# A selective-scan mixer kernel: old states enter through the first column of the products, most scans start from zero

## The chip, the cores and the metric

The kernel runs on one core of one Trainium2 chip. The metric is the device time of one execution in microseconds (us); the time before is the median of three executions. A trace of one further execution is what the rows below are read from.

The core has a matrix engine (TensorE, PE in the rows), a vector engine (VectorE, DVE), a scalar engine (ScalarE, ACT), GpSimd (POOL) and a queue that issues the transfers (SyncE, SP). Each runs its own instructions in the order in which they are written; semaphores make one wait for another.

## The reference

Three parts follow one another on an input of 4 sequences of 2048 tokens with 512 channels: a feed-forward part, the mixer, the same feed-forward part again, each with layer norm and a residual. The change lies in the mixer, cut here to what matters (D_INNER is 1024, D_STATE 16):

```
x, z = split((inp - mean(inp)) @ W_in)
x = silu(conv(x) + conv_b)
Bm, Cm = split(x @ W_x)
delta = softplus(x @ W_dt + b_dt)
def step(h, t):
    delta_t, B_t, C_t, u_t = t
    dA = exp(delta_t[:, :, None] * A[None, :, :])
    dBu = delta_t[:, :, None] * B_t[:, None, :] * u_t[:, :, None]
    h = dA * h + dBu
    y = einsum('bds,bs->bd', h, C_t)
out = ((y + x * D) * silu(z)) @ W_out
```

The state h (1024 channels by 16 states) is carried along the 2048 tokens of a sequence and starts at zero.

## The kernel before

The mixer cuts each sequence into 8 chunks of 256 tokens (T), so there are 32 chunks. A chunk has 8 blocks (ND) of 128 channels, which lie on the partitions, and a block has 4 units (NG) of 4 states (SG). A chunk is thus 32 units (NU), numbered n = 0 to 31; block b is units 4b to 4b+3. A unit is two pairs of states: the first pair (half 0) is scanned in place in PSUM, the second (half 1) is scanned from PSUM into SBUF (tile mx_hp).

What each engine does for a unit:

- ScalarE (decay, L1167) writes exp(delta * A) for a pair into one of three PSUM banks (mx_ps_da). A bank is free again when the pair three places earlier is done with: a first pair after VectorE has multiplied it by C (s_m2) and ScalarE has copied its last column to the state tile mx_hst (keep_psum, L1196), a second pair after its scan.
- GpSimd (times_b, L1009) writes delta*u*B for two units at a time into mx_dbu, which has room for four units (NM). So the products of units n and n+1 wait until unit n-3 is scanned.
- VectorE (scan, L1350) runs the recurrence along 256 tokens, four scans a unit, each starting from a column of mx_hst, or from the constant 0.0 in the first chunk of a sequence. It multiplies the first pair by C (times_c, L1363). It also does three taps of the convolution in each unit 4b (L1322) and the gating in each unit 4b+2 (L1330).
- GpSimd multiplies the second pairs of two units by C at once (times_c_sbuf, L1027; singly for the last four units), and per block adds two halves of delta (add_log, L996) and makes delta*u (delta_u, L1031).
- TensorE makes all products with weights and sums the states by transposes onto mx_ps_y.

For unit 4b+2 the first pair is different (on_pe): its products come from TensorE, and its decays go to mx_da_sb ahead of time.

All engines walk through the units with a written-out timetable. A list such as GATE_AT holds the unit at which the work for each block is due, counted from the chunk's unit 0, and the order in which the loops over due() stand is the order within that unit. Two silu visits a chunk, at units 5 and 21 (Z_SILU_AT), load the silu table, work on four blocks of z and of u, and load the exp table back (L1291, L1098, L1075, L1296). The B rows of the next chunk are loaded by SyncE in four transfers of 512 KB, one for each unit position g (spread, L900); the transfer for g is issued when the products of unit 28+g are made, and before the change unit 0 waits for g = 0 and 1 only.

## Time and profile before

| | |
|---|---|
| median of 3 executions | 5207.4 us (5206.98 to 5207.64) |
| the profiled execution's own time | 5209.97 us |
| its span in the trace | 5208.0 us |
| the mixer's chunks lie at | 715.0 to about 4598 us |
| busy over the span: PE, DVE, ACT, POOL | 94%, 87%, 74%, 72% |
| instructions | 83685 |

The busy shares are means over three parts. GpSimd is little used in the feed-forward parts and nearly always busy in the mixer, so the mixer has to be read by itself, chunk by chunk.

### The profile page before, as it was taken

The numbers are of one execution on the slowest core, as the hardware profiler recorded it, in microseconds if no ns is written. First come the engines' busy times: TensorE is split into PE (matmuls) and PEld (weight loads), VectorE is DVE, ScalarE is ACT, GpSimd is POOL, SyncE is SP. The second block draws the span as 40 slices with busy tenths as digits, with TensorE's granted clock in tenths as the row PEclk, the third lists the DMA queues.
The fourth block names the chain that finished last, engine by engine and source line by source line (L and its number), as shares of the span: only waits on it lengthen the run. The fifth ranks groups of instructions, "written<-read, shape, count | busy, mean of one in ns | idle before, by whom it ended". The sixth has DMA issues, their size and how long they took to land. (4 is left out here: it accounts for less than half of the span.)

```text
span 5208.0 us, 83685 instructions
## 1 busy us (share of the span) xinstructions
PE 4916.9 (94%) x25472; PEld 3971.2 (76%) x25472; DVE 4510.7 (87%) x7540; ACT 3849.1 (74%) x9976; POOL 3756.8 (72%) x1701
## 2 busy tenths in 40 slices
PE   8999989999999999999999999999999999979999
PEld 6777767777777777777777777777777777768887
DVE  6777669999999999999999999999899999977775
ACT  5556558888888888888888888888888888854443
POOL 1111059999999999999999999999999999931110
PEclk9999999999999999999999999999999999989999
DMA  3222231111111111111111111111111111211111
GB/s 83 91 80 81 102 110 46 46 46 48 58 53 55 46 46 46 46 46 46 46 51 54 46 46 54 58 54 50 46 46 46 46 46 46 66 58 53 65 57 41
DMA packets 154802, 292.21 MB, mean 56 GB/s; under 512 B 40688, under 2 KB 58096, under 8 KB 154352
## 3 DMA queue, kind: packets, MB, share of 16 engines
q1 hardware_dynamic: 154352, 286.82, 16.6%
q8 instruction: 208, 3.41, 0.3%
q14 instruction: 242, 1.98, 0.1%
HBM read 218.60 MB, written 68.18 MB: 55 GB/s over the span
## 5 line engine op out<-in xcount | busy, mean ns | idle before, releaser
L1009 POOL TENSOR_TENSOR mx_dbu<-mx_bs,mx_du 128x2048 f32<-128x2048 f32 (+2 forms) x513 | 2047.3, 3991 | 291.7 <-DVE mx_hp L1350 287.4
L1167 ACT ACTIVATE mx_ps_da<-mx_dl,mx_a 128x256 f32<-128x256 f32 x3584 | 1558.6, 466 | 72.9 <-DVE mx_hp L1350 39.9
L1350 DVE TENSOR_TENSOR_SCAN mx_hp<-mx_ps_da,mx_hst,mx_dbu 128x256 f32<-128x256 f32 x1792 | 1333.5, 744 | 215.3 <-ACT mx_ps_da L1167 213.6
L1027 POOL TENSOR_TENSOR mx_hp<-mx_hp,mx_cs 128x1024 f32<-128x1024 f32 (+1 forms) x576 | 1220.7, 2125 | 4.6 <-ACT mx_hst L1176 4.6
L1472 PE MATMUL mx_ps_m<-mx_u,mx_w_dt 128*128 128x256 f32 x4096 | 947.9, 385 | 93.6 <-ACT mx_duT L1148 67.8
L1350 DVE TENSOR_TENSOR_SCAN mx_ps_da<-mx_ps_da,mx_hst,mx_dbu 128x256 f32<-128x256 f32 x1344 | 937.9, 748 | 4.8 <-ACT mx_ps_da L1167 1.8
L1472 PEld LDWEIGHTS mx_ps_m<-mx_u,mx_w_dt 128*128 128x128 f32 x4096 | 759.6, 190 | 239.0 <-issue 136.2
L1363 DVE TENSOR_TENSOR mx_hc<-mx_ps_da,mx_cs 128x512 f32<-128x512 f32 x1024 | 696.0, 680 | 10.3 <-PE mx_ps_y L1502 8.3
L1502 PEld LDWEIGHTS mx_ps_y<-mx_ident,mx_hp 128*128 128x128 f32 x4096 | 511.0, 142 | 203.6 <-issue 114.8
L1502 PE MATMUL mx_ps_y<-mx_ident,mx_hp 128*128 128x128 f32 x4096 | 620.3, 274 | 8.4 <-POOL mx_hp L1027 8.4
L1502 PE MATMUL mx_ps_y<-mx_ident,mx_hc 128*128 128x128 f32 x4096 | 617.2, 273 | 4.1 <-DVE mx_gy L1330 3.9
L247 POOL TENSOR_TENSOR f_rstd<-f_ve,f_half 128x4 f32<-128x4 f32 x48 | 48.4, 1009 | 682.4 <-DVE f_ve L414 682.4
L1441 PE MATMUL mx_ps_m<-mx_hT,mx_w_in 128*128 128x259 f32 x2048 | 520.1, 399 | 5.9 <-POOL mx_ident L990 3.8
L1452 PE MATMUL mx_ps_m<-mx_hT,mx_w_in 128*128 128x256 f32 x2048 | 485.2, 379 | 4.4 <-DVE mx_u L1322 4.4
L1502 PEld LDWEIGHTS mx_ps_y<-mx_ident,mx_hc 128*128 128x128 f32 x4096 | 482.0, 142 | 5.2 <-DVE mx_gy L1330 5.0
L1482 PE MATMUL mx_ps_c<-mx_w_out,mx_gy 128*128 128x512 f32 x992 | 466.7, 593 | 0.0
L1441 PEld LDWEIGHTS mx_ps_m<-mx_hT,mx_w_in 128*128 128x128 f32 x2048 | 390.8, 200 | 74.9 <-issue 14.3
L1452 PEld LDWEIGHTS mx_ps_m<-mx_hT,mx_w_in 128*128 128x128 f32 x2048 | 388.1, 190 | 73.1 <-issue 14.8
L1196 ACT ACTIVATE mx_hst<-mx_ps_da 128x2 f32<-128x2 f32 x1022 | 173.1, 169 | 363.1 <-DVE mx_hc L1363 352.9
L1322 DVE SCALAR_TENSOR_TENSOR mx_u<-mx_ps_m,mx_cw,mx_u 128x256 f32<-128x256 f32 x768 | 364.4, 475 | 31.1 <-ACT mx_u L1069 30.4
L253 POOL TENSOR_TENSOR mx_w_in<-f_xhT 128x2048 f32<-128x2048 f32 x30 | 110.6, 3688 | 323.7 <-ACT f_xhT L303 323.7
L1350 DVE TENSOR_TENSOR_SCAN mx_ps_da<-mx_da_sb,mx_hst,mx_ps_da 128x256 f32<-128x256 f32 x448 | 309.4, 743 | 0.0
(134 smaller groups left out, 8349.3 us busy)
## 6 DMA issues: line engine op xcount, KB each, us to landing
mx_bs<-bc_scratch SPq DMA_DIRECT2D x128, 512.0 KB, 4.6
mx_cs<-bc_scratch SPq DMA_DIRECT2D x128, 512.0 KB, 3.7
mx_hT<-hT_scratch SPq DMA_DIRECT2D x32, 518.0 KB, 4.2
hT_scratch<-f_h2T SPq DMA_DIRECT2D x16, 1024.0 KB, 8.9
mx_xo<-xs_scratch SPq DMA_DIRECT2D x32, 512.0 KB, 3.7
x_scratch<-mx_xo SPq DMA_DIRECT2D x32, 512.0 KB, 2.9
f_x<-in_L_attn_inp SPq DMA_DIRECT2D x12, 1024.0 KB, 6.5
xs_scratch<-f_x SPq DMA_DIRECT2D x12, 1024.0 KB, 4.3
```

What stands on the lines that cost most here:

```text
L1009: G.tensor_tensor(dbu[:, n % NM:n % NM + k].rearrange("p n s t -> p (n s) t")[:, skip:, :], bs[:, g:g + k].rearrange("p n s t -> p (n s) t ...
L1027: G.tensor_tensor(h, h, cs[:, g:g + k, SD:SG, :], ALU.mult).then_inc(s_pr, k - 1 + step_to(n))
L1167: ins = A.activation(dst[:, k, :], dl[:, b % NL, :], ACT.Exp, scale=a_sb[:, b, s:s + 1])
L1196: A.activation(hst[:, b, SG * g:SG * g + SD], ps_da[DA_BANK[p]][:, :, T - 1], ACT.Copy).then_inc(s_kd, 1)
L1322: V.scalar_tensor_tensor(out=q, in0=in_bank(b)[:, step:step + T], scalar=cw[:, step, b:b + 1], in1=q, op0=ALU.mult, op1=ALU.add).then_inc( ...
L1350: ins = V.tensor_tensor_scan(bank if in_psum(p) else hp[:, n % NH, k, :], da, db, 0.0 if first else hst[:, b, SG * g + s:SG * g + s + 1], ...
L1363: V.tensor_tensor(hc[:, n % NC, :, :], ps_da[DA_BANK[2 * n]][:, :, :], cs[:, g, 0:SD, :], ALU.mult).then_inc(s_m2, 1)
L1441: ins = M.matmul(in_bank(b)[:, 0:TH], w_in_sb[:, f, b * P:(b + 1) * P], hT[cp][:, f, :], start=(f == 0), stop=(f == NB - 1))
L1452: ins = M.matmul(m_bank(b)[:, 0:T], w_in_sb[:, f, DI + b * P:DI + (b + 1) * P], hT[cp][:, f, PAD_L:PAD_L + T], start=(f == 0), stop=(f == ...
L1472: ins = M.matmul(m_bank(b)[:, 0:T], w_dt_sb[:, k, b * P:(b + 1) * P], u[:, cp, k, :], start=(k == 0), stop=(k == ND - 1))
L1482: ins = M.matmul(ps_c[:, :], gy[:, cp, b, j * P:(j + 1) * P], w_out_sb[:, b, :], start=False, stop=(b == ND - 1), skip_group_check=True)
L1502: ins = M.matmul(y_sum(b)[:, j * P:(j + 1) * P], pair[:, k, j * P:(j + 1) * P], ident[:, :], is_transpose=True, start=(first and k == 0 an ...
```

## The change

1. A scan starts from the constant 0.0 in all chunks, except for the first pair of units 4b+2, which still starts from mx_hst. The old state enters otherwise: the first column of mx_dbu becomes delta*u*B plus exp(delta*A) of the first token times the old state.
2. For that ScalarE makes, once a block, the 16 first decays (first_decays, tile e0, due at unit 4b-2), and GpSimd makes `carry` = e0 times the old states and `enter` = B times delta*u of the first token (carried, due at unit 4b-1), 16 elements each. In times_b a small addition fills column 0 and the product fills columns 1 to 255. `enter` reads all four B transfers.
3. ALL_IN_PSUM = (10, 11, 26, 27): in these four units the second pair is scanned in PSUM too and multiplied by C on VectorE (times_c_second), not on GpSimd.
4. On ScalarE the work due at units 4b+2 (relu) now stands behind the decays of the second pair; the silu visit stands ahead of other work of its unit. On VectorE the gating stands after the first pair's scans. On TensorE the turn of delta*u stands behind the sum of the SBUF states. The parts of the output product and its copies are due at other units, and the B/C product one unit later.

```
+            G.memset(hst[:, :, :], 0.0).then_inc(s_hz, 1)
-        OUT_AT = [NU - 6, NU - 2, NU + 2, NU + 10, NU + 13, NU + 14, NU + 15, NU + 18]
+        OUT_AT = [NU - 6, NU - 2, NU + 2, NU + 8, NU + 10, NU + 14, NU + 17, NU + 19]
-        ALL_IN_PSUM = ()
+        ALL_IN_PSUM = (10, 11, 26, 27)
+        E0_AT = [NG * b - 2 for b in range(ND)]
+        CARRY_AT = [NG * b - 1 for b in range(ND)]
...
+            def carried(c, b):
+                pool.wait_ge(s_e0, ND * c + (b + 1))
...
+                G.tensor_tensor(carry[:, b % 2, :], e0[:, b % 2, :], hst[:, b, :], ALU.mult).then_inc(s_cy, 1)
+                pool.wait_ge(s_du, ND * c + b + 1)
+                if b == 0:
+                    for g in range(NG):
+                        pool.wait_ge(s_bl[g], 16 * (c + 1))
+                G.tensor_tensor(enter[:, b % 2, :].rearrange("p (g s) -> p g s", g=NG), bs[:, :, :, 0],
+                                du[:, b % 2, 0:1].unsqueeze(1).to_broadcast([P, NG, SG]), ALU.mult).then_inc(s_cy, 1)
...
+                    if not first:
+                        pool.wait_ge(s_cy, 2 * (ND * i + b + 1))
...
+                if not first:
+                    states = slice(SG * g + skip, SG * (g + k))
+                    G.tensor_tensor(out[:, :, 0], enter[:, b % 2, states], carry[:, b % 2, states], ALU.add)
+                G.tensor_tensor(out[:, :, t0:], rows[:, :, t0:], bcast(du[:, b % 2, t0:], k * SG - skip),
+                                ALU.mult).then_inc(s_m1, k)
...
+            def first_decays(c, b):
+                act.wait_ge(s_dl, ND * c + (b + 1))
+                if not (is0(c) and b < 2):
+                    act.wait_ge(s_cy, 2 * (ND * c + (b - 1)))
+                A.activation(e0[:, b % 2, :], a_sb[:, b, :], ACT.Exp, scale=dl[:, b % NL, 0:1]).then_inc(s_e0, 1)
...
                         if on_pe(p):
-                            pass
+                            continue
...
-                        if half == 0:
+                        if half == 0 or on_pe(p - 1):
                             for bb, s in due(DT_AT, n, i, RELU):
                                 relu(i + s, bb)
...
-                                           0.0 if first else hst[:, b, SG * g + s:SG * g + s + 1], ALU.mult, ALU.add)
+                                           hst[:, b, SG * g + s:SG * g + s + 1] if on_pe(p) and not first else 0.0,
+                                           ALU.mult, ALU.add)
```

How the instructions stand now is shown at three places. First GpSimd over one block in the middle of a chunk, before: products of units 4b and 4b+1, states times C, delta's sum, products of 4b+2 and 4b+3, delta*u, states times C.

```order
L1009 TENSOR_TENSOR mx_dbu<-mx_bs,mx_du 128x2048
L1027 TENSOR_TENSOR mx_hp<-mx_hp,mx_cs 128x1024
L996 TENSOR_TENSOR mx_dl<-mx_dl,mx_en 128x256
L1009 TENSOR_TENSOR mx_dbu<-mx_bs,mx_du 128x1536
L1031 TENSOR_TENSOR mx_du<-mx_dl,mx_u 128x256
L1027 TENSOR_TENSOR mx_hp<-mx_hp,mx_cs 128x1024
```

The same block on GpSimd after the change:

```order
L1018 TENSOR_TENSOR mx_carry<-mx_e,mx_hst 128x16
L1023 TENSOR_TENSOR mx_enter<-mx_bs,mx_du 128x16
L1044 TENSOR_TENSOR mx_dbu<-mx_enter,mx_carry 128x8
L1045 TENSOR_TENSOR mx_dbu<-mx_bs,mx_du 128x8x255
L1062 TENSOR_TENSOR mx_hp<-mx_hp,mx_cs 128x1024
L1006 TENSOR_TENSOR mx_dl<-mx_dl,mx_en 128x256
L1044 TENSOR_TENSOR mx_dbu<-mx_enter,mx_carry 128x6
L1045 TENSOR_TENSOR mx_dbu<-mx_bs,mx_du 128x6x255
L1066 TENSOR_TENSOR mx_du<-mx_dl,mx_u 128x256
L1062 TENSOR_TENSOR mx_hp<-mx_hp,mx_cs 128x1024
```

Four small instructions came in; the two at the head stand directly in front of the block's first product and so behind everything of the block before.

Second, ScalarE from the end of a silu visit at unit 5, before: table load, relu of the next block, then the decays of unit 6's second pair, the copy of z and exp.

```order
L1296 ACT_TABLE_LOAD
L1132 ACTIVATE mx_en<-mx_ps_m,mx_bdt 128x256
L1133 ACTIVATE mx_dl<-mx_ps_m,mx_bdt 128x256
L1196 ACTIVATE mx_hst<-mx_ps_da 128x2
L1167 ACTIVATE mx_ps_da<-mx_dl,mx_a 128x256
L1167 ACTIVATE mx_ps_da<-mx_dl,mx_a 128x256
L1176 ACTIVATE mx_hst<-mx_hp 128x2
L1093 ACTIVATE mx_gy<-mx_ps_m 128x256
L1137 ACTIVATE mx_en<-mx_en 128x256
```

The same stretch of ScalarE after the change:

```order
L1327 ACT_TABLE_LOAD
L1242 ACTIVATE mx_hst<-mx_ps_da 128x2
L1213 ACTIVATE mx_ps_da<-mx_dl,mx_a 128x256
L1213 ACTIVATE mx_ps_da<-mx_dl,mx_a 128x256
L1171 ACTIVATE mx_en<-mx_ps_m,mx_bdt 128x256
L1172 ACTIVATE mx_dl<-mx_ps_m,mx_bdt 128x256
L1222 ACTIVATE mx_hst<-mx_hp 128x2
L1132 ACTIVATE mx_gy<-mx_ps_m 128x256
L1176 ACTIVATE mx_en<-mx_en 128x256
L1194 ACTIVATE mx_e<-mx_a,mx_dl 128x16
```

The decays moved ahead of relu, and the first decays of the next block came in as the last of the unit's work. Except for the table load the order is the same in every unit 4b+2.

Third, GpSimd at the end of a chunk after the change, from the products of units 30 and 31 to those of units 0 and 1 of the next chunk; before, the double product of units 26 and 27 stood ahead of the single one, and neither small instruction stood there.

```order
L1045 TENSOR_TENSOR mx_dbu<-mx_bs,mx_du 128x6x255
L1066 TENSOR_TENSOR mx_du<-mx_dl,mx_u 128x256
L1062 TENSOR_TENSOR mx_hp<-mx_hp,mx_cs 128x512
L1018 TENSOR_TENSOR mx_carry<-mx_e,mx_hst 128x16
L1023 TENSOR_TENSOR mx_enter<-mx_bs,mx_du 128x16
L1044 TENSOR_TENSOR mx_dbu<-mx_enter,mx_carry 128x8
L1045 TENSOR_TENSOR mx_dbu<-mx_bs,mx_du 128x8x255
```

The instruction at L1023 is the first that reads the next chunk's B rows, all four transfers of them.

## Rows read from the trace of the kernel before

**Rows 1.** Two chunks: busy us (count) of PE, PEld, DVE, ACT, POOL; clock; DMA share; GB/s.

```profile
2167.32:2289.26 121.94, 116.02 (x624) 93.87 (x624) 113.95 (x193) 100.28 (x283) 112.02 (x51) 0.99 0.15 49
2656.49:2775.97 119.48, 115.26 (x624) 93.76 (x624) 106.51 (x192) 99.76 (x283) 111.50 (x51) 0.99 0.15 50
```

**Rows 2.** Who waited for whom in chunk 2167.32 to 2289.26: us, times, longest.

```profile
POOL mx_dbu L1009 <- DVE mx_hp L1350: 9.7, 9, 2.7
DVE mx_hp L1350 <- ACT mx_ps_da L1167: 7.7, 3, 2.9
```

**Rows 3.** Scans with and without a state operand: duration ns min/median/max.

```profile
L1350 DVE TENSOR_TENSOR_SCAN mx_ps_da<-mx_ps_da,mx_hst,mx_dbu x1344: 732/748/779, 828.0 to 4588.0; 128x256 f32<-128x256 f32 x192
L1350 DVE TENSOR_TENSOR_SCAN mx_ps_da<-mx_ps_da,mx_dbu x192: 672/689/724, 715.0 to 3745.5; 128x256 f32<-128x256 f32 x192
```

**Rows 4.** VectorE's order of time (start us, us): units 4, 6, 8, 12.

```profile
2181.73 1.39 DVE L1350 TENSOR_TENSOR_SCAN mx_ps_da<-mx_ps_da,mx_hst,mx_dbu 128x256 f32<-128x256 f32 x2
...
2189.23 1.38 DVE L1350 TENSOR_TENSOR_SCAN mx_ps_da<-mx_da_sb,mx_hst,mx_ps_da 128x256 f32<-128x256 f32 x2
2193.24 0.75 DVE L1350 TENSOR_TENSOR_SCAN mx_hp<-mx_ps_da,mx_hst,mx_dbu 128x256 f32<-128x256 f32 x1 [2.63 <-ACT mx_ps_da L1167]
...
2198.64 1.38 DVE L1350 TENSOR_TENSOR_SCAN mx_ps_da<-mx_ps_da,mx_hst,mx_dbu 128x256 f32<-128x256 f32 x2
...
2212.78 1.39 DVE L1350 TENSOR_TENSOR_SCAN mx_ps_da<-mx_ps_da,mx_hst,mx_dbu 128x256 f32<-128x256 f32 x2
```

**Rows 5.** GpSimd's groups by shape: busy us, mean ns, idle before and releaser.

```profile
L1009 POOL TENSOR_TENSOR mx_dbu<-mx_bs,mx_du 128x2048 f32<-128x2048 f32 x255 | 1157.5, 4539 | 177.0 <-DVE mx_hp L1350 175.0 <-issue 1.7
...
L996 POOL TENSOR_TENSOR mx_dl<-mx_dl,mx_en 128x256 f32<-128x256 f32 x256 | 187.5, 732 | 46.0 <-ACT mx_en L1141 45.9
...
L247 POOL TENSOR_TENSOR f_rstd<-f_ve,f_half 128x4 f32<-128x4 f32 x48 | 48.4, 1009 | 682.4 <-DVE f_ve L414 682.4
```

**Rows 6.** GpSimd's order of time: products of units 8 and 12, then the block's rest.

```profile
2189.47 4.53 POOL L1009 TENSOR_TENSOR mx_dbu<-mx_bs,mx_du 128x2048 f32<-128x2048 f32 x1 [0.20 <-DVE mx_hp L1350]
...
2206.38 4.54 POOL L1009 TENSOR_TENSOR mx_dbu<-mx_bs,mx_du 128x2048 f32<-128x2048 f32 x1 [1.04 <-DVE mx_hp L1350]
2210.87 2.36 POOL L1027 TENSOR_TENSOR mx_hp<-mx_hp,mx_cs 128x1024 f32<-128x1024 f32 x1
...
2217.96 2.36 POOL L1027 TENSOR_TENSOR mx_hp<-mx_hp,mx_cs 128x1024 f32<-128x1024 f32 x1
```

**Rows 7.** All engines at unit 18: VectorE's start of it, ScalarE behind exp.

```profile
2236.96 1.37 DVE L1350 TENSOR_TENSOR_SCAN mx_ps_da<-mx_da_sb,mx_hst,mx_ps_da 128x256 f32<-128x256 f32 x2
...
2238.11 0.47 ACT L1167 ACTIVATE mx_ps_da<-mx_dl,mx_a 128x256 f32<-128x256 f32 x1
```

**Rows 8.** ScalarE's order of time through the silu visit at unit 5.

```profile
2184.76 0.17 ACT L1196 ACTIVATE mx_hst<-mx_ps_da 128x2 f32<-128x2 f32 x1
...
2191.40 0.47 ACT L1132 ACTIVATE mx_en<-mx_ps_m,mx_bdt 128x256 f32<-128x256 f32 x1
...
2192.13 0.17 ACT L1196 ACTIVATE mx_hst<-mx_ps_da 128x2 f32<-128x2 f32 x1
...
2193.81 0.86 ACT L1167 ACTIVATE mx_ps_da<-mx_dl,mx_a 128x256 f32<-128x256 f32 x2
```

**Rows 9.** GpSimd at the chunk's end: products of units 28 and 30.

```profile
2268.56 4.54 POOL L1009 TENSOR_TENSOR mx_dbu<-mx_bs,mx_du 128x2048 f32<-128x2048 f32 x1 [1.05 <-DVE mx_hp L1350]
...
2276.07 3.44 POOL L1009 TENSOR_TENSOR mx_dbu<-mx_bs,mx_du 128x1536 f32<-128x1536 f32 x1
```

**Rows 10.** B transfers: landing times of all, then the last of this chunk.

```profile
DMA to landing us min/median/max: 3.3/4.6/6.8
...
L900 SPq DMA_DIRECT2D mx_bs<-bc_scratch x1: 367/367/367, 2280.0 to 2280.0; - x1
...
DMA to landing us min/median/max: 6.7/6.7/6.7
```

**Rows 11.** ScalarE at unit 16: the wait for the input product.

```profile
2228.87 0.56 ACT L1069 ACTIVATE mx_u<-mx_ps_m,mx_cb,mx_cw 128x256 f32<-128x256 f32 x1 [3.42 <-PE mx_ps_m L1441]
```

More of the change, by code:

```diff
@@ L726, in mixer_phase @@
         yt = sb("yt", [P, 2, T])
+        e0 = sb("e0", [P, 2, DS])
+        carry = sb("carry", [P, 2, DS])
+        enter = sb("enter", [P, 2, DS])
         da_sb = sb("da_sb", [P, SD, T])
@@ L761, in mixer_phase @@
         s_m1 = sem("dbu_ready")
+        s_hz = sem("states_zeroed")
+        s_e0 = sem("first_decay_ready")
+        s_cy = sem("carry_ready")
         s_dut = sem("du_turned")
@@ L996, in add_log, with times_b @@
                 G.tensor_tensor(d, d, en[:, b % 2, :], ALU.add).then_inc(s_dl, 1)
-            def times_b(i, n, k):
+            def carried(c, b):
+                pool.wait_ge(s_e0, ND * c + (b + 1))
+                if not is0(c):
+                    pool.wait_ge(s_kd, NU * (c - 1) + NG * (b + 1))
+                    pool.wait_ge(s_st, NU * (c - 1) + last_in_sbuf(NG * (b + 1) - 1) + 1)
+                    if b == 0:
+                        pool.wait_ge(s_kdx, NE * (c - 1) + NE)
+                else:
+                    pool.wait_ge(s_hz, 1)
+                G.tensor_tensor(carry[:, b % 2, :], e0[:, b % 2, :], hst[:, b, :], ALU.mult).then_inc(s_cy, 1)
+                pool.wait_ge(s_du, ND * c + b + 1)
+                if b == 0:
+                    for g in range(NG):
+                        pool.wait_ge(s_bl[g], 16 * (c + 1))
+                G.tensor_tensor(enter[:, b % 2, :].rearrange("p (g s) -> p g s", g=NG), bs[:, :, :, 0],
+                                du[:, b % 2, 0:1].unsqueeze(1).to_broadcast([P, NG, SG]), ALU.mult).then_inc(s_cy, 1)
+            def times_b(i, n, k, first):
                 b, g = divmod(n, NG)
@@ L1008, in times_b @@
                 skip = SD if on_pe(2 * n) else 0
-                G.tensor_tensor(dbu[:, n % NM:n % NM + k].rearrange("p n s t -> p (n s) t")[:, skip:, :],
-                                bs[:, g:g + k].rearrange("p n s t -> p (n s) t")[:, skip:, :],
-                                bcast(du[:, b % 2, :], k * SG - skip), ALU.mult).then_inc(s_m1, k)
+                t0 = 0 if first else 1
+                out = dbu[:, n % NM:n % NM + k].rearrange("p n s t -> p (n s) t")[:, skip:, :]
+                rows = bs[:, g:g + k].rearrange("p n s t -> p (n s) t")[:, skip:, :]
+                if not first:
[3 more added lines that the diff above has]
+                                ALU.mult).then_inc(s_m1, k)
             def times_c(c, n):
@@ L1038, in prologue @@
                         delta_u(c, c, b)
+                    for b, c in due_before(CARRY_AT, n):
+                        carried(c, b)
             def body(i, par, first):
@@ L1042, in body @@
                     if is0(i) and n < 2:
-                        times_b(i, n, 1)
+                        times_b(i, n, 1, first)
                     elif n % 2 == 0:
-                        times_b(i, n, 2)
+                        times_b(i, n, 2, first)
                     for bb, s in due(DU_AT, n, i):
@@ L1049, in body @@
                         times_c(i + s, TIMES[m])
+                    for bb, s in due(CARRY_AT, n, i):
+                        carried(i + s, bb)
                     for bb, s in due(DT_AT, n, i, ADD):
@@ L1232, in prologue @@
                         A.preload_act_table_set("silu_and_others")
+                    for b, c in due_before(E0_AT, n):
+                        first_decays(c, b)
                     for b, c in due_before(DIAG_AT, n):
@@ L1272, in body @@
                         keep(i - 1, NU + n - KEEP_LAG)
+                    if due(Z_SILU_AT, n, i):
+                        A.preload_act_table_set("silu_and_others")
+                        for k, s in due(Z_SILU_AT, n, i):
+                            silu_z(i + s, (par + s) % 2, k)
+                        for k, s in due(U_SILU_AT, n, i):
+                            silu_u(i + s, (par + s) % 2, k)
+                        A.preload_act_table_set("natural_log_exp_and_others")
                     for bb, s in due(GATE_AT, n, i, ZCOPY):
@@ L1584, in body @@
                             last_out_product(j, range(2 * k, 2 * k + 2))
-                    for b, s in due(DU_TURN_AT, n, i):
-                        turn_du(i + s, b)
                     for b, s in due(DBU_AT, n, i):
@@ L1605, in body @@
                         sum_states(i - 1, NU + n - SUM_LAG)
+                    for b, s in due(DU_TURN_AT, n, i):
+                        turn_du(i + s, b)
                     if n >= SUMC_LAG:
```

17 lines of the change are left out of this document (6 added, 11 removed).

## The prediction

> **What bounds the kernel now.** I first read busy time by stretch. A chunk in the middle lasts 121.94 us, and the engines are busy for 116.0 (TensorE), 114.0 (VectorE), 112.0 (GpSimd) and 100.3 us (ScalarE) [rows 1]. Three engines are within 10 us of the period, so none can be read as the bound from its share; the waits decide. The list of waits for that chunk says that VectorE stands still for ScalarE's decays three times, 7.7 us together, and GpSimd stands still for VectorE's scans nine times, 9.7 us [rows 2]. So GpSimd follows VectorE: it is held by the rule that its products may overwrite a slot only when the unit three back is scanned. VectorE is the bound except around three places where ScalarE is late.
>
> VectorE's order of time shows both kinds of block. The block from unit 8 to unit 12 takes 14.14 us (2198.64 to 2212.78), without a wait; the block from unit 4 to unit 8 takes 16.91 us, of which 2.63 us are a stall behind the silu visit [rows 4]. GpSimd's order of time shows the cover that matters for this change. The product for units 8 and 9 starts at 2189.47, as soon as unit 5 is scanned, and lasts 4.53 us; VectorE wants it at 2198.64 [rows 4, 6]. In an undisturbed block the product for units 12 and 13 starts at 2206.38 and ends at 2210.92, and unit 12 starts at 2212.78: a cover of 1.86 us, no more [rows 4, 6].
>
> The last fact is from the first chunk of a sequence, whose scans already start from a constant. Its scans take 689 ns against 748 ns [rows 3], and VectorE is busy for 106.5 instead of 114.0 us, but the chunk takes 119.48 us, only 2.5 us less [rows 1]. Of each 3 us taken from VectorE, 2 came back as waits.
>
> **The change part by part.**
>
> *Scans from a constant.* 14 of a block's 16 scans lose 59 ns [rows 3]. VectorE's undisturbed block goes from 14.14 to 13.3 us, and its first two units from 7.50 us (2181.73 to 2189.23, eight scans) to 7.03 us [rows 4]. Per chunk that is 112 x 0.059 = 6.6 us less VectorE work.
>
> *Second pairs in PSUM.* GpSimd loses two double products, 2 x 2.31 us (2.36 less the 0.05 us by which the next instruction starts early) [rows 6]. VectorE gains four products of 512 columns. Each costs between nothing and a scan's 0.75 us; I take 0.6, so 2.4 us a chunk.
>
> *Small GpSimd instructions.* A later chunk gains 32: carry, enter and two additions per block. No like instruction is in the trace. Between 256 and 2048 columns the mean goes from 732 to 4539 ns, 2.12 ns a column [rows 5]; carried down to 8 or 16 columns that leaves 0.21 to 0.22 us, and 0.16 to 0.17 us from start to start. The bound from above is the 4-column instruction that takes 1009 ns [rows 5], but that one raises to a power. From below it is the slope alone, 0.02 to 0.03 us. I take 0.165, since the line fits multiplications and additions. The first product also waits for the `enter` just ahead of it: 0.15 us, from the 0.05 us of overlap that is lost and the delay of a release, which lies between 0 and the 0.24 us from unit 6's start to the product at 2189.47 [rows 4, 6]. The head of a block thus costs 0.17 + 0.17 + 0.15 + 0.16 = 0.65 us before the 4.54 us product. Columns 1 to 255 instead of 0 to 255 I cost at nothing.
>
> The Trainium skill gives another price: GPSIMD Engine Reference, Performance versus the Vector engine, counts about 2.6 cycles an element at 1.2 GHz and 4497 ns for 2048 elements. That leaves 60 ns besides the elements, so a small instruction would be about 0.08 us (an estimate from that page), and the sum below would be about 70 us lower. The trace agrees on the large one (4539 ns) and shows no small one.
>
> *The new wait for the first decays.* This is the part that decides. `carry` for block b waits for an exp that ScalarE does last in unit 4b-2. Queued behind that wait on GpSimd is the product for units 4b and 4b+1, which VectorE needs at unit 4b. Call D the start of a block on VectorE and T the start of its third unit, D + 7.03. Before, ScalarE reaches the place of the new exp at T + 1.15 (2238.11 less 2236.96) [rows 7]. Relu now stands behind the decays instead of filling ScalarE's wait ahead of them: 0.73 us (2191.40 to 2192.13) [rows 8]. With the exp at 0.2 us (the two-column copies take 0.17 [rows 8]) and 0.1 us for releases, GpSimd starts at T + 2.18. Then 0.65 + 4.54 + 0.05: VectorE can start the next block at D + 7.03 + 2.18 + 5.24 = D + 14.45. Its own work needs 13.3, so it waits.
>
> GpSimd's own way round is as long: from the end of the product 9.35 us of other work (2210.87 to 2217.96, and 2.31, less the overlap of 0.05), 0.16 for the second addition, and 0.65 + 4.54 give 14.7 us [rows 6]. A normal block after the change takes the longer of the two, 14.7, against 14.14 before.
>
> *Silu blocks.* ScalarE copies a state at 2184.76, 3.03 us after D, and is at the place of the exp at 2193.81 [rows 4, 8]. Three shorter scans bring that to D + 11.9. GpSimd, which before went ahead at 2189.47 (D + 7.7), now goes on at D + 12.15, and VectorE gets unit 8 at D + 17.4, against 16.91 before. Moving relu shortens the 2.63 us stall at unit 6, but unit 8 then waits instead: a stall that moves. For the second visit, whose stall was 0.3 us longer [rows 2, 4], I take 17.7.
>
> *The chunk's end.* `enter` for block 0 reads all four B transfers. From the end of the product for unit 28 to that of unit 30 it is 6.41 us, 6.57 with the addition [rows 9]. The last transfer is issued 0.5 us after that (2280.0) and lands 4.6 us later in the median, 6.7 in this chunk [rows 10]; I take 5.7 us from product to landing. Then 0.17 + 0.15 + 0.16 + 4.54 and 0.1: 6.57 + 5.7 + 5.1 = 17.4 us for the last block. The removed double product lies in this wait and gains nothing there.
>
> *Output product and turns.* At unit 16 ScalarE waits 3.42 us for TensorE's input product [rows 11]. One of the output parts ahead of it moves behind, and the blocks before it are longer, so I take this stall as gone: block 4 costs 14.7. TensorE's order else costs nothing: it was busy 116.0 us of 121.94 [rows 1] and the period grows. ScalarE's eight exps (1 us a chunk) hide in its 20 us of idle time.
>
> *The sum.* Block 0: 14.45 (its state products are single, so the exp decides). Block 1: 17.4. Block 2: 14.7. Block 3: 15.05 (only one double product, but a C product of 0.6 ahead of T). Block 4: 14.7. Block 5: 17.7. Block 6: 14.7. Block 7: 17.4. Together 126.1 us, 4.2 more than 121.94. There are 28 such chunks: +117 us. First chunks lack the additions and the wait for `enter`, some 2.5 us: 123.5 against 119.48, three times +4. The very first chunk (715.0 to 828.0 [rows 3]) also waits at its start for all B: +8, an estimate. In all +137 us. The profiled execution took 5209.97 us, 2.5 more than the median; on the median of 5207.4 this gives 5345.
>
> **The rivals.**
>
> *VectorE stays the bound (faster).* If the exp comes at least 1.2 us earlier than I work out, or the product is not needed at once, the cover holds. Then a block takes 13.3, a silu block 16.91 - 0.94 - 0.73 = 15.3, with 2.4 for the new products: 113 us, and GpSimd with 112.0 - 4.6 + 5.3 = 112.7 is beside it. With 3 us of waits left a chunk takes 116, and the kernel 5035. For it: the removed stall at unit 16 and 6.6 us of scans are real. Against it: the cover was 1.86 us, and the head of the block costs more than 2.7 us. Chance 0.15.
>
> *Gains and waits cancel.* With small instructions near 0.08 us, a release near nothing and landings of 5.1 us the sum of blocks is about 122.5, and the time 5200 to 5235. Chance 0.14, half of it within 0.2%.
>
> *Small GpSimd instructions are dear.* At 0.4 us each a block on GpSimd's way costs 4 x 0.24 more, 7.7 us a chunk, and the time is about 5560; at the 1.0 us of the power row it would be above 6000. It decides from about 0.25 us. Chance 0.08.
>
> *The scans do not get shorter.* The constant start is in the trace already [rows 3]. Then the blocks hardly change, since VectorE is not their bound: 5360 to 5400. Chance 0.03, within my forecast's range.
>
> The forecast itself, 5235 to 5470, has 0.60.
>
> **How the numbers follow.** 0.2% (10 us) is about what a measurement of this kernel can tell. Slower: 0.60 + 0.07 + 0.08 + 0.03 = 0.78. Same: 0.07. Faster: 0.15. The range runs from 5190, which leaves out the faster case, to 5470: the sum with 0.22 us a small instruction and landings of 7.2 us gives about 5440.
>
> **What would show it.** Scans at 689 ns outside units 4b+2. GpSimd idle ahead of `carry`, released by ScalarE's exp: 2 to 5 us in the silu blocks, little in the others; and 3 to 4 us ahead of the `enter` at a chunk's end, released by the B transfer. VectorE's stalls move from the second pairs at units 6, 16 and 22 to the first scans of units 8 and 24 and of unit 0, released by GpSimd's product. TensorE's busy time per chunk stays near 115 us. If VectorE's waits for GpSimd stay under 3 us a chunk, or small instructions take under 0.1 us, the forecast is wrong.

## The result, and the profile after

The changed kernel takes 5472.8 us in the median of 4 runs (5465.61 to 5484.1), the kernel before 5207.19 beside it: 1.0512 times as long, interval [1.0493, 1.0531]. The forecast was 5345 us, so the direction was right and the size half of what came: +265 us instead of +137. The measured time lies just above the range's end of 5470.

All profiles below are of the run of 5465.61 us. Its page, the span and the busy times:

```profile
span 5463.8 us, 85499 instructions
PE 4981.4 (91%) x25472; PEld 3959.1 (72%) x25472; DVE 4439.1 (81%) x7668; ACT 3909.8 (72%) x10232; POOL 3770.8 (69%) x2598
```

The span is 255.8 us longer than before. Where it grew is seen chunk by chunk. I took the start of the first scan of every fourth unit (those of units 0, 4, 8, ... of a chunk) from VectorE's order of time; the differences are the lengths of the eight blocks. The table has medians over 27 later chunks.

| block | 0 | 1 | 2 | 3 | 4 | 5 | 6 | 7 | chunk |
|---|---|---|---|---|---|---|---|---|---|
| before | 14.32 | 16.91 | 14.15 | 14.42 | 16.40 | 17.23 | 14.15 | 14.28 | 121.95 |
| forecast | 14.45 | 17.4 | 14.7 | 15.05 | 14.7 | 17.7 | 14.7 | 17.4 | 126.1 |
| after | 14.71 | 17.78 | 14.76 | 15.31 | 14.81 | 18.62 | 16.77 | 17.27 | 129.91 |

First chunks of a sequence take 126.99 us (before 119.48), the very first 126.02 (before 113.02). 28 x 7.96, 3 x 7.5 and 13 give 258 us, the span's growth to within 3 us.

The stretches that answer to [rows 1]: busy us (count) of PE, PEld, DVE, ACT, POOL, then the granted clock, DMA share, GB/s; a later chunk, and a first one.

```profile
2261.70:2391.75 130.05, 117.83 (x626) 93.02 (x625) 110.82 (x197) 102.17 (x290) 112.81 (x81) 0.99 0.14 46
2786.40:2913.30 126.90, 117.02 (x623) 93.97 (x622) 109.81 (x196) 102.40 (x290) 110.30 (x66) 0.98 0.13 47
```

VectorE is busy for 3 us less than in [rows 1] and GpSimd for 1 us more, and the chunk is 8 us longer. No engine became the bound by its work; what grew is waiting. The waits of that chunk, up to the start of the next chunk's first scan (us, times, longest), which answer to [rows 2]:

```profile
POOL mx_carry L1018 <- ACT mx_e L1194: 14.0, 6, 3.8
DVE mx_ps_da L1400 <- POOL mx_dbu L1045: 8.9, 6, 3.4
DVE mx_hp L1400 <- ACT mx_ps_da L1213: 5.5, 3, 2.0
DVE mx_ps_da L1400 <- ACT mx_ps_da L1213: 3.1, 3, 1.8
ACT mx_u L1108 <- PE mx_ps_m L1492: 4.1, 2, 3.6
```

Before, GpSimd waited for VectorE nine times; now it waits for ScalarE's new exp six times, 14.0 us. VectorE waits for GpSimd's product six times, 8.9 us, of which 3.4 are the wait at the chunk's end; in 3000 us of the mixer before it did so twice, 1.4 us in all. It still waits for the decays, now at first pairs too (three times before in the same 3000 us, 2.6 us). The last row, ScalarE waiting for TensorE's input product, is at another place than that of [rows 11], as shown below.

The scans (duration ns min/median/max, first and last start), to be set beside [rows 3]:

```profile
L1400 DVE TENSOR_TENSOR_SCAN mx_ps_da<-mx_ps_da,mx_dbu x1792: 668/675/699, 714.0 to 4843.3; 128x256 f32<-128x256 f32 x200
L1400 DVE TENSOR_TENSOR_SCAN mx_ps_da<-mx_da_sb,mx_hst,mx_ps_da x448: 727/730/755, 847.0 to 4840.0; 128x256 f32<-128x256 f32 x150
```

The small instructions, their products and VectorE's new one, from the groups by shape (busy us, mean ns | idle before them):

```profile
L1018 POOL TENSOR_TENSOR mx_carry<-mx_e,mx_hst 128x16 f32<-128x16 f32 x256 | 56.7, 221 | 445.8 <-ACT mx_e L1194 443.5 <-DMA mx_bs<-bc_scratch 1.6
L1023 POOL TENSOR_TENSOR mx_enter<-mx_bs,mx_du 128x16 f32<-128x16 f32 x256 | 57.2, 223 | 60.5 <-DMA mx_bs<-bc_scratch 60.5
L1044 POOL TENSOR_TENSOR mx_dbu<-mx_enter,mx_carry 128x8 f32<-128x8 f32 x224 | 46.8, 209 | 35.9 <-POOL mx_enter L1023 20.3 <-DVE mx_ps_da L1400 2.0 <-issue 0.9
L1045 POOL TENSOR_TENSOR mx_dbu<-mx_bs,mx_du 128x2040 f32<-128x2040 f32 x224 | 1012.7, 4521 | 0.0
L1423 DVE TENSOR_TENSOR mx_hx<-mx_ps_da,mx_cs 128x512 f32<-128x512 f32 x128 | 86.2, 674 | 0.0
```

The first group is `carry`, the second `enter`, the third the addition that fills the first column, the fourth the product behind it, and the last the second pairs' product on VectorE. A small GpSimd instruction takes 207 to 223 ns whether it has 6 or 16 columns, close to the 0.21 to 0.22 us to which the line of [rows 5] comes down; from start to start it is 0.16 to 0.18. The 443.5 us of idle time ahead of `carry` are the largest new wait.

**The second silu visit, where most of block 5's and 6's excess lies.** ScalarE's order of time (start us, us), from the table load before the visit on:

```profile
2344.55 1.28 ACT L1322 ACT_TABLE_LOAD   x1
...
2347.87 1.28 ACT L1327 ACT_TABLE_LOAD   x1
...
2349.37 0.87 ACT L1213 ACTIVATE mx_ps_da<-mx_dl,mx_a 128x256 f32<-128x256 f32 x2
...
2350.99 0.38 ACT L1132 ACTIVATE mx_gy<-mx_ps_m 128x256 f32<-128x256 f32 x1
2351.25 0.36 ACT L1157 ACTIVATE mx_ps_c<-mx_w_x 32x256 f32<-32x256 f32 x1
2351.56 0.40 ACT L1176 ACTIVATE mx_en<-mx_en 128x256 f32<-128x256 f32 x1
2351.86 0.29 ACT L1194 ACTIVATE mx_e<-mx_a,mx_dl 128x16 f32<-128x16 f32 x1
```

GpSimd in the same stretch (in brackets the idle time before and who ended it):

```profile
2352.37 0.22 POOL L1018 TENSOR_TENSOR mx_carry<-mx_e,mx_hst 128x16 f32<-128x16 f32 x1 [3.84 <-ACT mx_e L1194]
2352.55 0.22 POOL L1023 TENSOR_TENSOR mx_enter<-mx_bs,mx_du 128x16 f32<-128x16 f32 x1
2352.93 0.21 POOL L1044 TENSOR_TENSOR mx_dbu<-mx_enter,mx_carry 128x8 f32<-128x8 f32 x1 [0.16 <-POOL mx_enter L1023]
2353.09 4.52 POOL L1045 TENSOR_TENSOR mx_dbu<-mx_bs,mx_du 128x2040 f32<-128x2040 f32 x1
```

And VectorE behind it, the first and the second pair of unit 24:

```profile
2357.73 1.28 DVE L1400 TENSOR_TENSOR_SCAN mx_ps_da<-mx_ps_da,mx_dbu 128x256 f32<-128x256 f32 x2 [1.75 <-POOL mx_dbu L1045]
...
2360.71 0.69 DVE L1400 TENSOR_TENSOR_SCAN mx_hp<-mx_ps_da,mx_dbu 128x256 f32<-128x256 f32 x1 [1.70 <-ACT mx_ps_da L1213]
```

This is the forecast's chain to the letter: exp, `carry`, product, unit 24. The block had begun at 2339.08, so the exp is at D + 12.78 and unit 24 at D + 18.65. The head from `carry` to the product is 0.18 + 0.38 + 0.16 = 0.72 us, against the 0.65 forecast. From the exp to `carry` it is 0.51 us here and 0.44 in the median of this block (28 chunks, starts from the two orders of time); in the other blocks the median is 0.38 to 0.45.

At 2351.25 ScalarE does what the forecast had passed over: it clears the PSUM tile of the B/C product. TensorE waits for that. Its own order of time:

```profile
2349.08 0.60 PE L1553 MATMUL mx_ps_y<-mx_ident,mx_hc 128*128 128x128 f32 x4
2351.66 5.02 PE L1512 MATMUL mx_ps_c<-mx_u,mx_w_x 128*32 128x256 f32 x16 [1.98 <-ACT mx_ps_c L1157]
2356.61 1.58 PE L1492 MATMUL mx_ps_m<-mx_hT,mx_w_in 128*128 128x259 f32 x6
```

Behind the B/C product stands block 7's input product, ScalarE's convolution at unit 24 waits for it (the 3.6 us in the list of waits), and the decays stand behind the convolution: that is the 1.70 us at VectorE above. The exp for block 7 stands behind it too, at D + 10.96 in the median instead of D + 8.96 (D is the start of a block on VectorE, as in the prediction). The 16 multiplications take 5.02 us, where the same 16 took this in the kernel before:

```profile
2252.42 3.61 PE L1461 MATMUL mx_ps_c<-mx_u,mx_w_x 128*32 128x256 f32 x16 [0.48 <-ACT mx_u L1075]
```

The stretches after the change (length, PE busy, granted clock, DMA share, GB/s) show why:

```profile
2345.00:2349.60 4.60, 3.79 (x26) 1.00 0.37 114
2349.60:2351.60 2.00, 0.08 (x1) 0.87 0.00 0
2351.66:2353.60 1.94, 1.94 (x5) 0.50 0.00 0
2353.60:2356.60 3.00, 3.00 (x12) 0.85 0.00 0
```

TensorE worked at full clock, stood still for 2 us, and was then granted half of it (0.50, the level of 1.2 GHz) for the first seven or eight multiplications, 427 ns from one start to the next instead of 216. The wait of 2.0 us thus costs TensorE 3.4 here. The Trainium skill says that the halved clock is the state without activity and that work lifts it (TensorE: Matmul & The Clock Gate, Part 1: The HAM clock gate). The trace agrees: here the clock fell in the idle time (0.87 over that stretch), and it came back while TensorE worked (0.85 over the last stretch).

The fall doesn't come each time. TensorE waits about 2.0 us at this place in every later chunk, but the clock falls in 22 of the 27. The product then takes 5.2 us and block 6 takes 16.83 (medians). In the other five it stays at full clock and block 6 takes 15.29. In one of these five the product reads:

```profile
1448.01 3.64 PE L1512 MATMUL mx_ps_c<-mx_u,mx_w_x 128*32 128x256 f32 x16 [2.00 <-ACT mx_ps_c L1157]
```

So of the 2.07 us by which block 6 is over the forecast, the wait by itself makes some 0.6 and the slower clock behind it 1.5.

### The profile page after: what moved, and what is told of

Its sections match the earlier page's. It is cut to its first block and busy times, and to the rows that moved or that the text cites. A ratio compares the mean times of both kernels' runs of the same rounds, so it can differ in the third digit from the quotient of the medians.

```text
span 5463.8 us, 85499 instructions
## 1 busy us (share of the span) xinstructions
PE 4981.4 (91%) x25472; PEld 3959.1 (72%) x25472; DVE 4439.1 (81%) x7668; ACT 3909.8 (72%) x10232; POOL 3770.8 (69%) x2598
## 5 line engine op out<-in xcount | busy, mean ns | idle before, releaser
L1045 POOL TENSOR_TENSOR mx_dbu<-mx_bs,mx_du 128x1530 f32<-128x1530 f32 (+4 forms) x513 | 2038.9, 3975 | 4.3 <-issue 3.7
L1400 DVE TENSOR_TENSOR_SCAN mx_ps_da<-mx_ps_da,mx_dbu 128x256 f32<-128x256 f32 x1792 | 1150.5, 681 | 373.1 <-POOL mx_dbu L1045 144.7
L1400 DVE TENSOR_TENSOR_SCAN mx_hp<-mx_ps_da,mx_dbu 128x256 f32<-128x256 f32 x1792 | 1209.1, 675 | 175.9 <-ACT mx_ps_da L1213 174.3
L1062 POOL TENSOR_TENSOR mx_hp<-mx_hp,mx_cs 128x1024 f32<-128x1024 f32 (+1 forms) x512 | 1068.5, 2090 | 3.6 <-ACT mx_hst L1222 3.6
L1553 PE MATMUL mx_ps_y<-mx_ident,mx_hp 128*128 128x128 f32 x3584 | 550.2, 276 | 101.3 <-POOL mx_hp L1062 99.8
L1553 PEld LDWEIGHTS mx_ps_y<-mx_ident,mx_hp 128*128 128x128 f32 x3584 | 431.6, 141 | 270.0 <-POOL mx_hp L1062 171.4
L1492 PEld LDWEIGHTS mx_ps_m<-mx_hT,mx_w_in 128*128 128x128 f32 x2048 | 379.2, 194 | 117.2 <-ACT mx_dl L1172 34.2
L1503 PEld LDWEIGHTS mx_ps_m<-mx_hT,mx_w_in 128*128 128x128 f32 x2048 | 387.6, 189 | 72.9 <-issue 14.8
L1579 PE MATMUL mx_ps_da<-mx_bdiag,mx_duT 128*128 128x256 f32 x1024 | 280.5, 396 | 133.6 <-DVE mx_hp L1400 133.6
L1018 POOL TENSOR_TENSOR mx_carry<-mx_e,mx_hst 128x16 f32<-128x16 f32 x256 | 56.7, 221 | 445.8 <-ACT mx_e L1194 443.5
```

The costliest lines, as they stand in the source:

```text
L1045: G.tensor_tensor(out[:, :, t0:], rows[:, :, t0:], bcast(du[:, b % 2, t0:], k * SG - skip), ALU.mult).then_inc(s_m1, k)
L1062: G.tensor_tensor(h, h, cs[:, g:g + k, SD:SG, :], ALU.mult).then_inc(s_pr, k - 1 + step_to(n))
L1400: ins = V.tensor_tensor_scan(bank if in_psum(p) else hp[:, n % NH, k, :], da, db, hst[:, b, SG * g + s:SG * g + s + 1] if on_pe(p) and not ...
L1492: ins = M.matmul(in_bank(b)[:, 0:TH], w_in_sb[:, f, b * P:(b + 1) * P], hT[cp][:, f, :], start=(f == 0), stop=(f == NB - 1))
L1503: ins = M.matmul(m_bank(b)[:, 0:T], w_in_sb[:, f, DI + b * P:DI + (b + 1) * P], hT[cp][:, f, PAD_L:PAD_L + T], start=(f == 0), stop=(f == ...
L1553: ins = M.matmul(y_sum(b)[:, j * P:(j + 1) * P], pair[:, k, j * P:(j + 1) * P], ident[:, :], is_transpose=True, start=(first and k == 0 an ...
```

## The experiments

Each block value below is the median over later chunks, read as in the table above. The runs e1, e2 and e4 each undo or shift one thing in the changed kernel, e3 two, and nothing of the computation is left out in any run.

**e1: the first decays one unit earlier.**

```diff
-        E0_AT = [NG * b - 2 for b in range(ND)]
+        E0_AT = [NG * b - 3 for b in range(ND)]
```

and the call of `first_decays` ahead of the unit's silu visit.

> The changed kernel, but ScalarE makes block b's first decays at unit 4b-3, ahead of the silu visit, and no longer at the end of unit 4b-2. Theory A (the wait of GpSimd's carry for the first decays, and the product queued behind it, set the block's length): the silu blocks 4 to 8 and 20 to 24 fall from 17.8 and 18.6 us to about 16, blocks 0 and 12 by about 1 us each, normal blocks stay at GpSimd's own 14.7; some 5 to 6 us a chunk, so about 5290 us. Rival B (what costs is GpSimd's work itself, or TensorE's order): within 20 us of 5473.

It took 5307.35 us (1.0191 [1.0162, 1.0221]), 165 less than the changed kernel: 5290 was close. Blocks 1, 3, 5 and 7 lost 1.83, 1.41, 1.84 and 2.26 us, but block 0, expected to lose 1, hardly moved (14.63), and block 6 grew by 1.4 (18.18): TensorE's wait for the clearing is now 3.2 us a chunk instead of 2.0. The waits of the whole run:

```profile
POOL mx_carry L1018 <- ACT mx_e L1194: 62.1, 51, 5.4
DVE mx_hp L1400 <- ACT mx_ps_da L1213: 306.8, 151, 5.4
POOL mx_enter L1023 <- DMA mx_bs<-bc_scratch: 98.6, 32, 6.6
PE mx_ps_c L1512 <- ACT mx_ps_c L1157: 98.7, 31, 3.2
```

Idle time ahead of `carry` fell from 443.5 to 62.1 us. So the new wait is shown to be the main cause: it is worth 165 of the 265 us, though 380 us of idle time went, since VectorE's wait for the decays rose from 174.3 to 306.8 and TensorE's for the clearing from 62.0 to 98.7.

**e2: block 0's `enter` in two halves**, so that the head of a chunk wants two of the four B transfers.

```diff
-                    for g in range(NG):
+                    for g in range(2):
...
+                if n == 2:
+                    entering(0, 2, NG).then_inc(s_e2, 1)
```

> The changed kernel, but for block 0 enter is made in two halves: units 0 and 1 where it stood, waiting for the first two B transfers, and units 2 and 3 just ahead of the product for unit 2. One more small GpSimd instruction a chunk. Theory A (the wait for the fourth B transfer costs at the chunk's end): block 28 to 32 falls from 17.3 to about 15.0 us, where the first decays hold it; about 5405 us. Rival B (the first decays hold the carry there anyway): block 7 stays above 16.5 us and the time above 5450.

5425.34 us (1.0418 [1.0388, 1.0448]), 20 more than expected. Block 7 fell from 17.27 to 15.47, by 1.8 us where 2.3 were expected, and block 0 took 0.85 back (15.56). The time fell by 47 us. The two blocks account for 27 of them and the first chunks for 7; some 11 come from block 6, where TensorE's clock fell in 16 of 27 chunks instead of 22, so they belong to no wait for a transfer.

**e3: the B/C product and its clearing where they were.**

```diff
-        BC_AT, CLEAR = [-9], -1
+        BC_AT, CLEAR = [-10], -1
```

and the silu visit back at the end of its unit. The product at unit 22, its clearing at unit 21 and the visit behind the clearing: that is the order before, and the run doesn't tell its two edits apart.

> The changed kernel with the B/C product due at unit 22 again, its clearing at unit 21, and the silu visit at the end of its unit as before. Theory A (TensorE's product at unit 23 now waits for ScalarE's clearing behind the silu visit and makes the next input product, the first tap and unit 24 late, which my forecast did not have): blocks 20 to 24 and 24 to 28 fall from 18.6 and 16.8 to about 18.2 and 14.8 us, 2.4 us a chunk, about 5400 us. Rival B (those two blocks are long by what comes after the second silu visit whatever the order): within 20 us of 5473.

5412.94 us (1.0394 [1.0364, 1.0424]). Block 6 fell from 16.77 to 14.75, the forecast's own value; block 5 did not move (18.62). TensorE's wait for the clearing, 62.0 us in the whole changed kernel, is gone from the list, and the convolution's wait went from 131.6 to this:

```profile
ACT mx_u L1108 <- PE mx_ps_m L1492: 29.9, 41, 2.6
```

The exp of block 7 is back at D + 8.96. The B/C product takes 3.61 us again behind a wait of 0.47 and at full clock in all later chunks. The excess of block 6 is therefore the moved product with its clearing behind the silu visit, 60 us. That of block 5 is not: the exp stands at D + 12.76 instead of D + 12.80.

**e4: relu ahead of the decays again.**

```diff
-                            continue
+                            pass
...
-                        if half == 0 or on_pe(p - 1):
+                        if half == 0:
```

> The changed kernel with relu ahead of the decays of the second pair in units 4b+2 again. Theory A: the first decays come 0.7 us sooner in normal blocks, so blocks 0 and 12, which they hold, lose up to 0.7 us each, the blocks that GpSimd's own 14.7 us hold lose nothing, and the stall at units 6 and 22 grows by 0.7 us without cost, since unit 8 and 24 wait for the product anyway: 1 to 1.5 us a chunk, about 5435 us. Rival B (the new order helps): 5490 or more.

5393.7 us (1.0357 [1.0311, 1.0403]), 79 less than the changed kernel and 41 less than expected. Blocks 0 and 3 lost 0.7 us each, as expected, and block 6 lost 1.82, which was not. Most of that is the clock. TensorE waits as long for the clearing as before (2.02 us), but its clock fell in 6 of the 27 chunks instead of 22. Like beside like, block 6 takes 16.39 against 16.83 with a fall and 14.79 against 15.29 without one, so relu's place is worth 0.4 to 0.5 us there. Sixteen falls fewer, at 1.5 us each, are 24 of the 79 us. Whether relu's place made them fewer is not shown: the two executions, 5383.63 and 5403.77 us, differ by nearly as much, at mean granted clocks of 0.991 and 0.988. e3 leaves neither wait nor fall, so what e4 takes from block 6 is part of what e3 takes, and they don't add.

**e5: e1 to e4 together.**

> The changed kernel with the first decays early (as in e1), enter in halves (e2), the B/C product and the silu visit back (e3) and relu first (e4), all four. Theory A (the scheme itself is sound, and its cost is the place of its new waits): a chunk of 118 to 121 us, about 5150 us, faster than before the change. Rival B (GpSimd's added work and VectorE's added products eat the shorter scans whatever the order): 5220 or more.

5159.2 us (0.9906 [0.9889, 0.9922]), faster than before. The four alone saved 165 + 47 + 60 + 79 = 352 us; less 28 x 1.8 for the shared block 6 that gives 5171, and 5159 was measured. These four, each of them a place in the order or a wait, hold all of the loss. That the sum comes so close is in part chance, since e1's saving has in it the 1.4 us that block 6 gained, which e3 takes away.

**e6: e5 without the four second pairs in PSUM.**

```diff
-        ALL_IN_PSUM = (10, 11, 26, 27)
+        ALL_IN_PSUM = ()
```

> e5 with ALL_IN_PSUM empty, so GpSimd multiplies all second pairs by C again. Theory A (GpSimd's way round a block is then the bound): 4.6 us more GpSimd work and 2.4 us less VectorE work a chunk, blocks 12 to 16 and 28 to 32 some 0.8 to 1.5 us longer, about 60 us above e5. Rival B (VectorE is the bound): up to 70 us below e5.

5124.18 us (0.9837 [0.9821, 0.9854]), 35 below e5 and the fastest of all, where theory A had expected a loss of 60; rival B had up to 70 less. The waits and the busy times of the chunk that answers to the one above:

```profile
DVE mx_hp L1411 <- ACT mx_ps_da L1224: 6.0, 2, 3.1
DVE mx_ps_da L1411 <- POOL mx_dbu L1056: 2.7, 3, 1.3
```

```profile
2135.33:2254.15 118.82, 114.17 (x624) 92.59 (x624) 108.00 (x192) 101.79 (x291) 117.44 (x84) 1.00 0.15 50
```

GpSimd is busy for 117.44 of 118.82 us: once the waits are gone, it bounds the chunk. That doesn't rest on the share alone. Blocks 3 and 4 take 14.77 and 14.76, and blocks 1 and 2 together 29.56, twice 14.78: this is GpSimd's own way round, 14.7 in the forecast. Blocks 2 and 6 take 13.32, which is the forecast's 13.3 for an undisturbed VectorE; there it makes up for its stall in the silu block ahead. e5 has 4.5 us less work on GpSimd (113.0 a chunk) and 1.9 more on VectorE (110.0), and is slower: there VectorE's work and its waits for the decays set the chunk, and GpSimd waits for VectorE.

**The three parts alone, put into the kernel before.** e7 has only the changes of order, e8 only the four second pairs (`ALL_IN_PSUM = (10, 11, 26, 27)`), e9 only the scheme of first columns; e10 is the changed kernel without the second pairs.

> The kernel before with only the change's order: output parts and copies, B/C product at unit 23, relu behind the decays in units 4b+2, silu visit ahead, gating and turn of delta*u moved. Theory A: the stall at unit 16 goes (2.1 us a chunk), those at 6 and 22 shrink by 0.7 us each, and the B/C product's wait for its clearing makes unit 24 up to 2 us late: 1 to 2 us a chunk less, 5145 to 5185 us. Rival B (the order alone is slow): 5220 or more.

5282.11 us (1.0143 [1.0126, 1.016]): the theory that the order alone is a gain, 5145 to 5185 us, fell. Block 6 takes 17.81 (14.15 before), with the wait seen above:

```profile
PE mx_ps_c L1461 <- ACT mx_ps_c L1118: 92.2, 31, 3.3
ACT mx_u L1069 <- PE mx_ps_m L1441: 166.5, 143, 5.3
```

> The kernel before with only ALL_IN_PSUM = (10, 11, 26, 27). Theory A (VectorE bounds the blocks of the kernel before): four more products of 0.6 us, 2.4 us a chunk, about 5280 us. Rival B (GpSimd's relief pays): 5210 or less.

5342.71 us (1.0258 [1.0241, 1.0275]), 135 more than before where 73 were expected. Blocks 2, 3, 6 and 7 grew by 0.63, 0.65, 0.63 and 0.58 us, which is the new product of 674 ns on VectorE, less some overlap. Blocks 0 and 4 grew by 1.25 and 0.96 as well, in new stalls of 1.04 and 0.83 us at units 1 and 17 on ScalarE's decays; why these come up is not settled. GpSimd, which lost two double products a chunk, only idles longer (287.4 before):

```profile
POOL mx_dbu L1009 <- DVE mx_hp L1350: 536.7, 305, 4.3
```

> The kernel before with only the scans from zero, first decays, carry, enter and the first-column additions; second pairs and order as before. Theory A (the new waits set the blocks; relu stands first, so 14.0 in block 0, 14.7 where GpSimd's own way round decides, 17.8 and 18.3 in the silu blocks, 17.2 at the chunk's end where the B transfer decides): about 126 us a chunk, 5340 us. Rival B (the shorter scans pay by themselves): 5200 or less.

5393.7 us (1.0361 [1.0343, 1.0378]), +186 where 5340 was expected; the chunk takes 127.04, against 126 expected. Its silu blocks are 17.64 and 18.19, its last 17.16. So the scheme alone brings the wait for the exp and, behind it, VectorE's for the product (the first two lines) and that for the B transfers (the third):

```profile
POOL mx_carry L1018 <- ACT mx_e L1194: 251.1, 129, 10.7
DVE mx_ps_da L1400 <- POOL mx_dbu L1045: 192.3, 139, 8.1
POOL mx_enter L1023 <- DMA mx_bs<-bc_scratch: 33.1, 32, 1.7
```

> The changed kernel with ALL_IN_PSUM empty. Theory A (VectorE waits in most blocks, so four products of 0.6 us more or less on it cost only where they stand ahead of the exp, block 12 to 16, and GpSimd's relief hides in the wait for B): 10 to 30 us below the changed kernel. Rival B (the second pairs cost what they cost alone in e8, 135 us): about 5340 us.

5444.1 us (1.0453 [1.0436, 1.0471]), 29 less than the changed kernel, as theory A had it. Alone the second pairs cost 135 us, in the changed kernel 29, in the mended one 35. In e8 the four blocks with the product grow by 2.5 us a chunk and the two with the stalls by 2.2. In the changed kernel block 3 has most of the cost (15.31 against 14.76); the others wait anyway. From e6 to e5, blocks 0, 2, 4 and 6 grow by 1.06, 0.61, 0.40 and 0.61, and blocks 3 and 7, where GpSimd is relieved, lose 0.85 and 0.60.

**e11: e6 with relu behind the decays**, as in the change.

> e6 with relu behind the decays of the second pair, as the change has it. Theory A (with the first decays early nothing waits for what stands behind relu, and the stalls at units 6 and 22 shrink by 0.7 us each): 30 to 45 us below e6, about 5085 us. Rival B (relu releases TensorE's next input product, so the next tap comes late): 5130 or more.

5137.12 us (0.9863 [0.9847, 0.988]), 13 above e6; the expected 5085 was wrong, and rival B's 5130 or more is what came, though not shown to come by its mechanism. The median chunk is the same (118.81), since GpSimd bounds it, but ten of the 27 take 119.4 to 120.4, and first chunks 120.01 against 118.12. In nine of the ten TensorE's clock fell at the end of block 1, and block 2 then takes 15.14 to 15.31; in the 18 chunks without a fall there it takes 13.53 to 13.75, and e6 has no such fall at all. TensorE in the same place of a long and of a usual chunk (length, PE busy, granted clock, DMA share, GB/s):

```profile
1808.00:1811.30 3.30, 3.30 (x14) 0.59 0.00 0
2284.00:2288.10 4.10, 4.10 (x22) 1.00 0.00 0
```

**e12: e7 with the B/C product back** (e3's edit).

> e7 (the kernel before with the order alone), but the B/C product at unit 22, its clearing at unit 21 and the silu visit at the end of its unit as before. Theory A (the loss of e7 is TensorE's wait for the clearing and what it makes late at unit 24; the rest of the order gains): block 24 to 28 falls from 17.8 to about 14.2 us, 3.6 us a chunk, about 5165 us, below the kernel before. Rival B (relu behind the decays or the output parts lose): 5230 or more.

5185.49 us (0.9962 [0.9949, 0.9976]), 97 less than e7 and 22 less than before, where 5165 was expected. Block 6 is back at 14.16; the median of block 2 is 1.2 us longer (15.32), which was not expected. That too goes with the clock: block 2 takes 15.32 to 15.43 in the 17 chunks in which it fell at the end of block 1, and 14.16 in the other ten. Block 0 takes 16.3 in the 11 chunks in which it fell there, and 14.6 in the other 16. The rest of the order is a gain, and the move of one product had turned it into a loss.

## Why the prediction was half right

*What bounds the kernel.* Right: the waits decided, and 3 us less work on VectorE bought nothing. The scheme alone (e9), which takes 6 us from VectorE (107.9 a chunk), lost 186 us.

*Scans from a constant.* Right: 675 to 681 ns in the mean, 730 with a state operand. The 59 ns that were taken off are 55 to 60.

*Second pairs.* Taken at 0.6 us on the path; 0.58 to 0.65 in the four blocks of e8, but in the changed kernel mostly block 3 pays it (e10). The product itself takes 674 ns. That GpSimd's saved work "gains nothing" at the chunk's end holds too: block 7 takes 17.27 with it and 17.13 without it (e10).

*Small instructions.* Taken at 0.165, measured 0.16 to 0.18 from start to start; the wait of the addition for `enter` was taken at 0.15 and is 0.2 (0.38 from start to start against 0.18). The head costs 0.72 instead of 0.65. So both of the rivals' prices, 0.08 us and 0.4 us or more, are out.

*The new wait.* The mechanism and both silu blocks are as worked out, and e1 shows it. The exp stands where the forecast had it: at D + 11.89 in block 1 (11.9), at D + 8.96 in a normal block (7.03 + 1.88 = 8.91). Mis-sized is the way on: 0.38 to 0.45 us from exp to `carry`, where I had 0.25 to 0.3. With the head's 0.07 and some 0.05 at the product's end this gives the 0.26 us by which blocks 0 and 3 are over, and 0.3 of the 0.38 of block 1.

*The second silu visit, 17.7 against 18.62.* Here the exp stands at D + 12.80 and not at D + 12.2. I had put the first visit's distance, D + 11.9, there plus 0.3 us. In the kernel before, ScalarE reached this place at D + 12.40 in the second visit and D + 12.08 in the first, so the 0.3 was right, and the 12.2 were the 12.40 less the 0.18 of three shorter scans. These are the first decay of the block, the copy of an output part, the clearing and the decays at the place of the exp, before, in a block that began at 2243.60:

```profile
2243.64 0.88 ACT L1167 ACTIVATE mx_ps_da<-mx_dl,mx_a 128x256 f32<-128x256 f32 x2
2244.55 0.58 ACT L1112 ACTIVATE mx_xo<-mx_ps_c 128x512 f32<-128x512 f32 x1
2248.60 0.36 ACT L1118 ACTIVATE mx_ps_c<-mx_w_x 32x256 f32<-32x256 f32 x1
2256.00 0.86 ACT L1167 ACTIVATE mx_ps_da<-mx_dl,mx_a 128x256 f32<-128x256 f32 x2
```

And the first decay of the block after, which began at 2339.08:

```profile
2339.49 0.88 ACT L1213 ACTIVATE mx_ps_da<-mx_dl,mx_a 128x256 f32<-128x256 f32 x2
```

So the copy and the clearing stood ahead of the place before, too, and are not what came on top. ScalarE has only 0.22 to 0.25 us of idle time between the block's first decay and the exp, before and after, so shorter scans can't bring it forward: the 0.18 were taken off without ground. And it now begins the block's decays 0.43 us behind VectorE's start instead of 0.04. Together 0.57 of the 0.60. In e9, with the order before, the exp stands at D + 12.46, so that some 0.34 go with the order; which of its moves makes them isn't shown. The 0.60 us, 0.19 for the release and 0.13 from `carry` to unit 24 are the 0.92 of this block.

*Block 6, 14.7 against 16.77.* This is the step that failed, "TensorE's order else costs nothing: it was busy 116.0 us of 121.94 and the period grows". I judged an engine by its share where I had warned of it for the others. The moved clearing came behind the silu visit and the decays, TensorE stood still for 2.0 us ahead of a product that block 7's input product stands behind, and in 22 of 27 chunks its clock fell. e3 takes 2.02 us away, e7 brings 3.66 to the kernel before, e12 takes that off again: 58 us of the 128 that the forecast fell short; without them the time would lie in the range.

*The chunk's end, 17.4 against 17.27.* Right in size, and e2 shows that the transfers cost there. But GpSimd stands still for 1.7 us ahead of `enter` in the median, where I had 3 to 4: at that place `carry` has already waited 1.7 us for the exp, so the two waits share the end of the chunk, and without the transfers' only 1.8 us go.

*Unit 16.* Right: block 4 takes 14.81, forecast 14.7. The 3.6 us wait of ScalarE is a new one, at unit 24, and belongs to the B/C product.

*First chunks.* Taken at +4 each and +8 for the very first; +7.5 and +13. They are 2.9 us shorter than later chunks (forecast 2.5), and so carry the same errors.

Of the 128 us, block 6 has 58, block 5 has 26, the small terms of the other six blocks 26, and first chunks 15: 125 in all.

*The signs.* GpSimd's idle time ahead of `carry` is 2.9 and 3.8 us in the silu blocks, as forecast, but also 2.8 ahead of block 4's, where I had little. TensorE's busy time per chunk is 117.8 us and not near 115, in part since it works at the lower clock for some of it.

*The rivals.* That VectorE stays the bound would need the exp early, and e5 has that, without the moved clearing and the wait for the last transfers. It is also the run with the second pairs, as in this rival. GpSimd's work per chunk was right: 113.0 us, where I had 112.7. But the kernel takes 5159 and not 5035, and the chunk 119.9 and not 116: VectorE is busy for 110 us and waits for the decays for 8.3 us in one chunk, and I had left 3 us for all waits. e6 comes nearest, 5124 us, and there GpSimd fills 117.4 us of a chunk, since it has the second pairs' products back.
